# Layer 0 of a four-layer graph network: columns of 128 consecutive edges, dense tiles ordered behind the writes

## The reference

```python
Wh = h @ W + b                                   # 3125 x 64
row, col = (edge_index[0], edge_index[1])        # src, dst
sc = softplus(deg_coeff[0] * deg_v + deg_coeff[1])
sim = sum(Wh[row] * Wh[col]) / max(|Wh[row]| * |Wh[col]|, EPS)
base = adj_v * sc * (row != col)
prop_pos = segment_sum((base * relu(sim))[:, None] * Wh[col], row)
prop_neg = segment_sum((base * -relu(-sim))[:, None] * Wh[col], row)
out = scale * (coeff[0] * prop_pos + coeff[1] * prop_neg + coeff[2] * Wh)
```

## Time and profile before

| | us |
|---|---|
| runs | 5688.84, 5696.48, 5698.95 (median 5696.48) |
| profiled execution | 5697.31 |
| its span, first to last instruction | 5695.6 |
| zeroing issued / first write | 15.5 / 147.4 |
| merging on DVE | 60.5 to 778 |
| nodes; one-hot count | 779 to 863; 863 to 1022 |
| last write | 1187.4 |
| first tile's work on DVE / result of the last tile read | 1202.7 / 1524.0 |

### The profile page before, as it was taken

One profiled execution on the slowest core, in us unless ns is written; L12 is line 12 of the kernel. 1 busy time (PEld: TensorE's weight loads), 2 busy tenths in 40 slices (PEclk: granted clock), 3 DMA queues, 4 the chain that ended last, 5 costly groups with the idle time before them and its releaser, 6 DMA issues.

```text
span 5695.6 us, 60196 instructions
## 1 busy us (share of the span) xinstructions
PE 2580.8 (45%) x8833; PEld 1211.4 (21%) x8833; DVE 4391.7 (77%) x11920; ACT 762.9 (13%) x1961; POOL 3560.6 (63%) x3631
## 2 busy tenths in 40 slices
PE   0000022047677710000555555555577777736993
PEld 0000012012256610000322122222233333312332
DVE  8899979159879999765577777774688878889992
ACT  0000000013200000454022222221000000002331
POOL 0777777720067788776577777772677777724651
PEclk9999999988779965555577878775799989968995
DMA  9000017134244433887255655651799999937980
GB/s 358 4 2 2 2 44 283 59 134 150 78 172 161 158 132 115 311 301 242 70 175 182 182 182 179 183 163 47 270 310 310 308 309 307 310 114 257 332 309 16
DMA packets 464764, 1028.64 MB, mean 181 GB/s; under 512 B 142937, under 2 KB 258063, under 8 KB 434724
## 3 DMA queue, kind: packets, MB, share of 16 engines
q1 hardware_dynamic: 160026, 509.52, 24.8%
q10 hardware_dynamic: 172682, 300.27, 14.7%
q0 software_dynamic: 131840, 216.96, 13.9%
HBM read 552.59 MB, written 470.64 MB: 180 GB/s over the span
## 4 chain that ended last, share of the span: by engine, by line
POOL 37%; issue 22%; DVE 17%; PE 14%; DMA 6%; DVEq 2%; ACT 1%; POOLq 0%; SPq 0%; ACTq 0%
POOL arena L622 22%; POOL weights L651 14%; PE psum L1148 4%; PE psum L1149 4%; DMA arena<-tab,ring 4%; PE psum L1199 3%; DVE arena L1495 2%; DVE arena L1504 2%; DVE arena L1470 1%; PE psum L982 1%; DVE arena L1957 1%; DVE arena L1786 1%; DVE arena L1698 1%; POOL agg L642 1%; DVE arena L1790 1%
## 5 line engine op out<-in xcount | busy, mean ns | idle before, releaser
L622 POOL DMA_INDIRECT arena<-tab,ring x2352 | 2341.9, 996 | 717.4 <-issue 700.6
L1148 PE MATMUL psum<-arena,ident 128*128 128x512 f32 x1176 | 760.5, 734 | 763.7 <-DMA arena<-tab,ring 518.5
L1470 DVE SCALAR_TENSOR_TENSOR arena<-arena,ns 128x64 f32<-128x64 f32 (+2 forms) x2351 | 869.5, 370 | 305.8 <-issue 121.6
L651 POOL DMA_INDIRECT weights<-ring x784 | 802.2, 1023 | 381.6 <-issue 381.6
L1149 PE MATMUL psum<-arena,ident 128*128 128x512 f32 x1176 | 713.1, 693 | 0.0
L1148 PEld LDWEIGHTS psum<-arena,ident 128*128 128x128 f32 x1176 | 254.3, 232 | 1180.1 <-issue 856.9
L968 PE MATMUL psum<-ident,hst 128*64 128x128 f32 x175 | 43.3, 409 | 878.1 <-DVE hst L1376 878.1
L1342 DVE SCALAR_TENSOR_TENSOR arena<-arena,base 128x280 f32<-128x280 f32 (+1 forms) x784 | 382.7, 488 | 52.3 <-issue 31.4
L716 POOL TENSOR_TENSOR arena<-arena,score 128x256 f32<-128x256 f32 x294 | 232.5, 815 | 280.8 <-DMA arena<-spill 127.1
L611 POOL DMA_INDIRECT put<-arena,zidx x75 | 74.0, 987 | 529.7 <-DVE arena L1548 399.3
L1199 PE MATMUL psum<-arena,ident 128*128 128x512 f32 x784 | 362.2, 608 | 68.9 <-DVE arena L1957 68.4
(11 more groups left out here) (344 smaller groups left out, 3949.9 us busy)
## 6 DMA issues: line engine op xcount, KB each, us to landing
put<-zero SPq DMA_DIRECT2D x98, 1040.0 KB
arena<-put SPq DMA_DIRECT2D x98, 1040.0 KB, 7.6
spill<-arena ACTq DMA_DIRECT2D x98, 1024.0 KB, 5.4
arena<-spill SPq DMA_DIRECT2D x98, 1024.0 KB, 7.7
state<-arena ACTq DMA_DIRECT2D x147, 512.0 KB
put<-zero ACTq DMA_DIRECT2D x14, 3584.0 KB
arena<-put SPq DMA_DIRECT2D x98, 512.0 KB, 3.7
weights<-zero SPq DMA_DIRECT2D x1, 44800.0 KB, 130.7
```

The lines of the kernel that those rows point to most:

```text
L622: pool.indirect_dma_start(out=rows[:, h, k, :], out_offset=None, in_=table[:, :], in_offset=bass.IndirectOffsetOnAxis(ap=ring[:, h, word + ...
L651: pool.indirect_dma_start(out=weights0[:, :], out_offset=bass.IndirectOffsetOnAxis(ap=ring[:, u, k:k + 1], axis=0), in_=ringf[:, u, K + k: ...
L1148: pe.matmul(place, lhsT=ident[:, :], rhs=rows_of[0][:, s, columns, 0:width], start=True, stop=False)
L1470: beats.add(dve.scalar_tensor_tensor(out=rows[:, s, k, :], in0=before, scalar=mark(ns, g, k), in1=rows[:, s, k, :], op0=ALU.mult, op1=ALU. ...
```

## The change

- Edges of layer 0 are loaded in blocks. A column is now 128 consecutive edges (one per partition) and the columns follow `dst`. The loads have edges along the free axis, 112 partitions x 7 blocks x 128; the keys and weights are worked out in that form and PE turns them into columns. `PIECES` grows from 3 to 7 (`PB` = 112 columns each), the tiles from 28 to 32, `weights0` to 52.4 MB. A piece row takes the column's first node, whose edges may begin in the column before.
- Duplicates are sought in a column, not across 280 columns. For each 4 columns PE spreads the keys (a transpose of a broadcast column, into PSUM), DVE compares them with its own key under a triangular mask and writes a bf16 matrix, and PE multiplies that with the weight, split in three bf16 parts.
- `add0` is written out for all 14 windows and reads `words0` in place, so the ring copies are gone. The 7 gathers of piece rows stand behind window 5.
- Tiles are taken in the order in which their rows are complete (`ORDER`). SP reads for each node tile the number of windows that it needs (`due`, from the edge counts) and waits for that many. There are three `cells` buffers, not four.
- SP, not ACT, clears the later layers' tables: four windows behind the writes, ten between tile loads.
- Merging now comes first on DVE, ahead of what prepares the later layers, and so ahead of the second `softplus`, behind which ACT's parameter loads stand.
- `bend0` writes into PSUM, `similarity0` reads it there, and PE's dot products wait for `similarity0` two chunks back instead of `bend0`. `Wh` is kept in node order and scaled for all 32 tiles at once.

```diff
-SPANS = ((0, 5 * W), (5 * W, 4 * W), (9 * W, 5 * W))
-WIDEST = 5 * W
-PIECES = len(SPANS)
+PB = 112
+PIECES = T // PB
+ORDER = sorted(range(NT + T // PB), key=lambda t: (t + 1) / NT if t < NT else (t - NT + 1) / (T // PB))
...
+            def clear_window(w):
+                clear_columns(sp, put1, w * W, W, 1, zero_out)
+                clear_columns(sp, put2, w * W, W, GW, zero_out)
+            for w in range(4):
+                sp.wait_ge(added[GW - 1], w * 16 * K + 16 * K)
+                clear_window(w)
+            sp.wait_ge(due_set, 1)
+            for at, tile in enumerate(ORDER):
+                if at % 3 == 0 and 4 + at // 3 < NW:
+                    clear_window(4 + at // 3)
+                if at >= 3:
+                    sp.wait_ge(summed0, at - 2)
+                if tile < NT:
+                    last = sp.value_load(due[0:1, tile * 5 + 4:tile * 5 + 5], min_val=16 * K, max_val=NW * 16 * K)
+                else:
+                    last = (tile - NT + 1) * (PB // W) * 16 * K
                 for u in range(GW):
-                    if late(w, 1):
-                        sp.wait_ge(added[u], w * 16 * K)
-                    sp.dma_start(ring[:, u, :], words0[:, bass.ds(w * GW + u, 1), :]...).then_inc(ring0_in[u], 16)
...
+                    sp.wait_ge(added[u], last)
+                sp.dma_start(cells[:, at % 3, :], weights0[0:CELLS, :]...[tile * P:tile * P + P, :]).then_inc(cells_in[at % 3], 16)
...
             def add0(w):
+                ready((apart, w * 2 + 3))
                 for u in range(GW):
-                    ready((ring0_in[u], w * 16 + 16))
+                    if w:
+                        ready((added[u], w * 16 * K))
+                    g = w * GW + u
                     for k in range(K):
-                        pool.indirect_dma_start(..., ap=ring[:, u, k:k + 1], in_=ringf[:, u, K + k:K + k + 1], ...)
+                        pool.indirect_dma_start(..., ap=words0[:, g, k:k + 1], in_=words0f[:, g, K + k:K + k + 1], ...)
             pool.wait_ge(zero0_out, 16)
-            add0(0)
-            with pool.Fori(1, NW) as w:
+            for w in range(NW):
                 add0(w)
-            ready((tab_out, 16))
-            for piece in range(PIECES):
-                hold(0, tab0, wh[:, NT + piece, :], piece)
+                if w == 5:
+                    ready((tab_out, 16))
+                    for piece in range(PIECES):
+                        hold(0, tab0, wh_unit[:, NT + piece, :], piece_dst[:, piece:piece + 1])
...
+            def spread_keys(u, h):          # PE
+                if late(u, 2):
+                    pe.wait_ge(alike_set, u - 1)
+                for k in range(4):
+                    mm = pe.transpose(bank(h)[:, k * P:(k + 1) * P], over(key[:, bass.ds(u * 4 + k, 1)], P, P), ident[:, :])
+                mm.then_inc(spread0, 1)
+            def pass_on(u, h):              # PE
+                pe.wait_ge(alike_set, u + 1)
+                if late(u, 2):
+                    pe.wait_ge(taken0, u - 1)
+                for k in range(4):
+                    mm = pe.matmul(bank(2 + h)[:, k * 3:k * 3 + 3], lhsT=alike[:, h * 4 + k, :], rhs=parts0[:, bass.ds(u * 4 + k, 1), :]...)
+                mm.then_inc(gained, 1)
...
+            def mark_alike(u, h):           # DVE
+                dve.wait_ge(spread0, u + 1)
+                if late(u, 2):
+                    dve.wait_ge(gained, u - 1)
+                for k in range(4):
+                    column = bass.ds(u * 4 + k, 1)
+                    marked = dve.scalar_tensor_tensor(out=alike[:, h * 4 + k, :], in0=bank(h)[:, k * P:(k + 1) * P], scalar=key[:, column],
+                                                      in1=upper[:, :], op0=ALU.is_equal, op1=ALU.mult, accum_out=later[:, column])
+                marked.then_inc(alike_set, 1)
+            def take_gains(u, h):           # DVE
+                dve.wait_ge(gained, u + 1)
+                dve.tensor_reduce(gain[:, bass.ds(u * 4, 4)], bank(2 + h)[:, 0:12]..., AX.X, ALU.add).then_inc(taken0, 1)
...
-                if j * 4 + c >= 2:
-                    pe.wait_ge(bent, j * 4 + c - 1)
+                n, tile = at * 4 + c, ORDER[at]
+                if n >= 2:
+                    pe.wait_ge(work0, n - 1)
...
+            for at in range(TILES):         # DVE
+                weigh0(at, 0)
                 for c in range(4):
-                    if late(j, 1):
-                        bend0(j - 1, c)
-                    weigh0(j, s, uses, c)
-                    if late(j, 1):
-                        similarity0(j - 1, (s - 1) % 4, c)
+                    bend0(at, c)
+                    if c < 3:
+                        weigh0(at, c + 1)
+                    similarity0(at, c)
```

More of the change, by code:

```diff
@@ L131, in quads, with windows @@
         body(g, g % 4, (g // 4, g // 2))
+def windows(engine, body):
+    body(0)
+    with engine.Fori(1, NW) as w:
+        body(w)
 def units(engine, body):
@@ L336, in gnn_program @@
         added = [sem(f"added{u}") for u in range(GW)]
[L337 removed]
+        cells_in = [sem(f"cells_in{s}") for s in range(3)]
         ds_in, beta_out = sem("ds_in"), sem("beta_out")
@@ L1078, in _ @@
             for half in range(2):
[L1079 removed]
+                side = slice(half * D, half * D + D)
+                by_place = total0[side, :].rearrange("d (p i) -> d i p", i=NT)
                 for i in range(NT):
[L1081 to L1088 removed]
+                    mm = pe.matmul(bank(0, 4)[side, i * D:(i + 1) * D], lhsT=by_place[:, i, :], rhs=ident[side, side], start=True, stop=True)
@@ new lines, in _ @@
+            dve.wait_ge(consts, 10)
+            dve.wait_ge(blocks_in, 16 * 20)
+            src_blocks, dst_blocks = (tile[0:PB, :].rearrange(by_block, p=P) for tile in (src_b, dst_b))
+            step(dve.tensor_scalar(degt, degt, par[0:PB, 0:1], par[0:PB, 1:2], ALU.mult, ALU.add))
+            step(dve.scalar_tensor_tensor(out=logt, in0=degt, scalar=-1.0, in1=degt, op0=ALU.mult, op1=ALU.max))
+            dve.sem_inc(plus_in, 1)
+            step(dve.tensor_copy(dstf, dst_blocks))
+            step(dve.tensor_copy(keyt, src_blocks))
@@ new lines, in _, with columns @@
+            step(dve.scalar_tensor_tensor(out=baset, in0=degt, scalar=0.0, in1=logt, op0=ALU.max, op1=ALU.add))
+            tally.done(dve.tensor_tensor(baset, baset, adjt, ALU.mult), blocks_set)
+            def columns(tile, n):
+                dve.wait_ge(columns_up, n + 1)
+                step(dve.tensor_scalar(tile[:, 0:4 * PB], bank(2 * n)[:, 0:4 * PB], 1.0, None, ALU.mult))
+                step(dve.tensor_scalar(tile[:, 4 * PB:T], bank(2 * n + 1)[:, 0:T - 4 * PB], 1.0, None, ALU.mult))
@@ L1259, in _ @@
+            windows(dve, merge_window)
+            dve.wait_ge(edges_in, 16 * 11)
             step(dve.tensor_copy(dext, ints))
@@ L1506, in edges0 @@
-            def edges0(j, s, uses):
-                for c in range(4):
-                    if late(j, 1):
-                        bend0(j - 1, c)
-                    weigh0(j, s, uses, c)
-                    if late(j, 1):
-                        similarity0(j - 1, (s - 1) % 4, c)
-            tiles(dve, edges0)
-            for c in range(4):
-                bend0(TILES - 1, c)
-                similarity0(TILES - 1, (TILES - 1) % 4, c)
+                tally.done(dve.tensor_copy(piece_rows[:, :, half, :], wh_unit[:, NT:TILES, :]), piece_up)
```

389 lines of the change are left out of this document (193 added, 196 removed).

## The result

| | before | after |
|---|---|---|
| median of 4 runs each, us | 5695.96 (5688.84 to 5698.95) | 5455.07 (5454.06 to 5458.83) |
| ratio | | 0.9579, 95% interval 0.9565 to 0.9594 |
| profiled execution / its span | 5697.31 / 5695.6 | 5454.14 / 5452.2 |

What follows compares the result with a forecast made beforehand. Layer 0 was taken as two serial parts, POOL's 784 writes, then DVE's 28 tiles. Overlapped, last write 1244, three tiles behind, end 1294 before 1524.0; less 1.5 for closing, gain 228.5 from 5697.3: 5469 us, range 5425 to 5560.

Steps and rivals of the forecast that it cites:

- one-hot stretch: Layer 0's one-hot count lengthens the writes beside it: 0.222 us on each of 107, 24 us, unchanged by the change.
- tiles' stretch: Writes beside 29 of 32 tiles are lengthened by `weigh0`, two writes a chunk: 42 us, bounds 0 and 125.
- nodes, edges, scaling: Long two-input DVE instructions of nodes, edge preparation and scaling of 32 tiles lengthen writes: 15 us estimated.
- last write to the copy of the sums: End of layer 0: landing, load and SP to 1254, three tiles 36.6, drain 3; from 1244 to 1294.
- closing part more than before: End of layer 0: 50 closing transposes for 24 cost 1.5 us more.
- Forecast A: The forecast itself, with its terms at either end: 5430 to 5520 us; chance 0.70.
- B: Rival: tiles stretch writes more, through PSUM-input instructions or full DMA queues: 5552, up to 5620 us; chance 0.15.
- E: Rival: overlap doesn't come off, a tile's load passes only with the last window: about 5780 us; chance 0.02.
- C: Rival: no stretching by tiles (the skill's rule) and zeroing at 138 us: 5420 us; chance 0.08.
- Start of the writes: Start of layer 0: zeroing issued at 18.5 takes 145 us, first write at 165, 17 us later; bounds 158 and 172.
- Pitch: POOL's 784 writes: 0.958 plus 0.30 us each, 1.262, for descriptors; merging no longer stretches; two a chunk beside tiles, 1.41.
- Tile start: First tile at 701 us, merge unit (4 columns) 1.7, bounds 1.3 and 2.8 (PE at half clock); not in the sum.

Runs made afterwards that it cites:

- PSUM run: In the one-hot row, the kernel of the three edits, whose one-hot comparison reads its row of places from PSUM: 5425.22 against 5700.45 of the kernel before.
- serial: Changed kernel, but every tile load waits for all 784 writes: 5778.81 us against 5695.44 of the kernel before, first kind of chip, single runs.
- PSUM `weigh0`: Changed kernel, but `weigh0` takes its first operand from PSUM and waits for its chunk's `bend0`; weights not the reference's: 5414.56 us, kernel before 5695.44.
- three edits: Changed kernel with zeroing ahead of edge loads, one-hot places read from PSUM, sums copied in PE's reading order: 5425.22 us, kernel before 5700.45.
- n = 8: Changed kernel, first tile load waiting until 8 of 14 windows are written: 7857.19 us, ratio 0.9975 to the kernel before, second kind of chip.

## Why the prediction was right, step by step

| term | predicted | measured |
|---|---|---|
| first write | 165 | 148.8 |
| 784 writes at 1.262, 7 gathers | 989 + 9 | 989 + 10.5 (0.958 a write and 238.7 between them; 8.4 + 2.1) |
| one-hot stretch | 24 | 26.8 (PSUM run) |
| tiles' stretch | 42 | 45.0 (serial and PSUM runs) |
| nodes, edges, scaling | 15 | 7 (the rest) |
| last write | 1244 | 1226.6 |
| last write to the copy of the sums | 50 | 50.2 |
| closing part more than before | 1.5 | 9.4 |
| layers 1 to 3 | 0 | -5.5 |

- **Mechanism.** Right: two serial parts became one, three tiles stand behind the last write, and the end is last write + 50. That held in three kernels whose last writes came at 1226.6, 1181.8 and 1193.2: 50.2, 51.7 (PSUM `weigh0`) and 49.9 us (three edits). Forecast A, not B or E. C, no stretching at all, falls with the 45 and 26.8 us.
- **Start of the writes: the mis-sized step.** "By size 149.4 us", cut to 145, measured 130.9. The old transfer was taken as a rate of its own, 351 GB/s, though parameter loads shared its queues; the prediction saw them and took off 4 us where 18 were due. That is 14 of the 16 us by which the first write was missed, and an issue at 17.0 in place of 18.5 is nearly all of the rest; the whole was missed by 15.
- **Pitch.** Right in size and in cause. Merging does not stretch writes (144 took 137.59, 0.955 each), tiles do by `weigh0` alone. The predicted two writes a chunk (1.41) read 1.43 from 650 to 900.
- **Tile start.** 701 predicted, 642.5 measured: a merge unit took 288/196 = 1.47 us for 1.7, and DVE stood 32.5 us for the parameter loads in place of 50. Neither was in the sum. DVE had caught up by 892 (939.42 - 47.44), not near 1000. With 403 in place of 390 the tiles would decide from a start at 874; this margin of 231 us is worked out, not run. The bound of 2.8 us a unit at PE's half clock did not come either: in the serial run the granted clock was 0.53 over the merging, and it took the same time.

```profile
42.00:330.00 288.00, 230.57 (x1560) 162.31 (x1559) 246.93 (x1802) 0.00 (x0) 137.34 (x144) 0.53 0.45 178
```

- **Closing transposes: missed.** The code was read as "50 for 24"; it is 50 f32 products, 0.25 us each, for 24 transposes and two products, 0.13 each on average.
- **Layers 1 to 3.** 4158.95 us behind L1597 after, 4164.5 before; the same code took 4162.8 to 4166.4 in the serial, the PSUM and the three-edit kernel, so 5.5 us is about what executions differ by.

The misses were -16.2 at the start, -1.2 in the writes, +7.9 in the closing and -5.5 behind it: -15 together. The -1.2 is in part luck: gathers, one-hot and tiles cost 7 us more than predicted, the other preparation 8 less.

## What to carry to other kernels

Where a producer on one engine and a consumer on others stand in series, order the consumer's work by when its input is complete, and price the end as the later of (last piece + what must follow it) and (consumer's start + all its work); only the larger counts, and the rest is slack, as long as the consumer can start early enough. Then look at what the new neighbours do to the pacing engine: here one operand moved from SBUF to PSUM was worth 27 us, and another some 40 in a kernel that forms other weights; with the right ones it is untested. A transfer's rate is that of everything on its queues; before scaling it by size, look at what ran beside it.

## What the runs showed of the hardware that was not expected

- The chip matters as much as the kernel: the kernel before took 5695 to 5700 us on some and 7874 to 7941 on others, and a 4.2% gain was 0.25% there. In layer 0, 748 us of it, it is DVE's 10 us waits beside indirect DMAs (copy of the sums at 2025.2 for 1276.75); the larger part lies behind layer 0, where such waits stand too (25 of L1645 are 208.8 us with n = 8; 0.8 us for its equal on the first kind) but were not added up. Why these chips do so is open.
- A multiplication with the unit matrix as a transpose costs about two and a half times a transpose of the same 64x64 block (6.3 against 2.5 us for 25).
- One DMA from a zeroed tile ran at 420 GB/s with nothing beside it, in pieces of 3584 as of 4096 bytes, and at 408 in pieces of 3200. The kernel before lost time on it from when other loads ran beside it, down to 169 GB/s in the last 12 us (290 in the changed one).
